# Transposing the doubled attention output once per tile, with the gate weights spread by DMA, in a two-layer Trainium2 block

## The reference

```python
rw = _gating(hidden_states, sim_matrix, gates)        # (b, t, 16)
q = einsum('bte,bted->btd', rw, einsum('btc,ecd->bted', h, q_proj))   # k and v likewise
scores = where(causal, einsum('bqd,bkd->bqk', q, k) * scale, -inf)
attn = einsum('bqk,bkd->bqd', softmax(scores, axis=-1), v)
mixed = attn[:, :, None, :] * rw[..., None]           # (b, t, 16, 64)
return einsum('bted,edc->btc', mixed, o_proj)
```

## Time and profile before

| | |
|---|---|
| median of 3 runs | 1398.0 us (1397.77 to 1398.74) |
| the profiled execution | 1397.29 us, of it 1395.1 us span |
| mean granted clock of PE over the span | 0.972 (1.00 in all of the second layer's tiles past the first) |
| busy over the span | PE 87%, DVE 86%, ACT 79%, POOL 73% |
| first matmul of the tiles | 1093.3 us from the span's start |

### The profile page before, as it was taken

The page is one execution under the profiler, slowest core; times in us unless marked ns, Lnnn a source line. Parts: engine busy times, 40 slices in busy tenths (PEclk is TensorE's granted clock), DMA queues, the critical chain, the costliest instruction groups (busy, mean ns, idle before and its releaser), DMA issues. The chain is left out here.

```text
span 1395.1 us, 24022 instructions
## 1 busy us (share of the span) xinstructions
PE 1208.1 (87%) x8370; PEld 753.3 (54%) x8370; DVE 1196.0 (86%) x1937; ACT 1107.6 (79%) x2031; POOL 1024.6 (73%) x714
## 2 busy tenths in 40 slices
PE   2789999999999999999999999998862599999997
PEld 1344444444454444454444445444431498989897
DVE  5899999999999999999999999999858576767674
ACT  3899999999999999999999999999833455656553
POOL 3689899899989989998998999899942744434320
PEclk9899999999999999999999999999975799999999
DMA  4232111121211112121111212110003876768570
GB/s 112 68 89 66 40 44 52 31 56 44 62 47 39 52 31 57 42 65 51 33 52 31 59 45 61 31 31 1 1 7 55 151 130 120 137 113 146 100 130 10
DMA packets 184598, 86.85 MB, mean 62 GB/s; under 512 B 150176, under 2 KB 166048, under 8 KB 184480
## 3 DMA queue, kind: packets, MB, share of 16 engines
q1 hardware_dynamic: 184480, 85.33, 28.9%
HBM read 7.68 MB, written 2.10 MB: 7 GB/s over the span
## 5 line engine op out<-in xcount | busy, mean ns | idle before, releaser
L490 POOL TENSOR_TENSOR prob<-prob 128x1024 f32<-128x1024 f32 x256 | 604.0, 2359 | 88.4 <-ACT prob L954 72.4
L1245 DVE TENSOR_REDUCE negmax<-score_ps 128x1 f32<-128x1024 f32 x512 | 621.3, 1220 | 35.3 <-PE score_ps L609 26.2
L925 ACT ACTIVATE prob<-score_ps,negmax 128x1024 f32<-128x1024 f32 x512 | 569.8, 1120 | 52.5 <-DVE negmax L1245 47.3
L609 PE MATMUL score_ps<-ka,qa 128*128 128x512 f16 x1024 | 308.3, 383 | 92.6 <-ACT prob L925 81.1
L638 PE MATMUL attn_ps<-probT,v_sb 128*64 128x512 f32 x1024 | 275.9, 618 | 0.8 <-ACT attn_nT L972 0.8
L632 PE MATMUL trans_ps<-ident,prob 128*128 128x128 f32 x2048 | 268.9, 274 | 2.7 <-POOL prob L490 2.7
L632 PEld LDWEIGHTS trans_ps<-ident,prob 128*128 128x128 f32 x2048 | 239.0, 141 | 57.3 <-POOL prob L490 4.0
L557 POOL TENSOR_TENSOR xs<-xnT,rw_all 128x2048 f32<-128x2048 f32 x32 | 117.4, 3671 | 147.3 <-DVE prob L1378 140.5
L488 POOL TENSOR_SCALAR prob<-prob,ccol 128x1024 f32<-128x1024 f32 x192 | 215.0, 1120 | 3.4 <-DVE ccol L1258 3.4
L609 PEld LDWEIGHTS score_ps<-ka,qa 128*128 128x128 f16 x1024 | 88.5, 98 | 211.9 <-ACT prob L925 179.6
L332 DVE COPY probT<-trans_ps 128x512 f32<-128x512 f32 x256 | 174.2, 681 | 3.1 <-PE trans_ps L632 3.1
(11 more groups left out here) (195 smaller groups left out, 1327.9 us busy)
## 6 DMA issues: line engine op xcount, KB each, us to landing
qa<-split SPq DMA_DIRECT2D x256, 64.0 KB, 2.0
ka<-split SPq DMA_DIRECT2D x256, 64.0 KB, 2.0
xg<-xnT SPq DMA_DIRECT2D x16, 512.0 KB, 3.0
resid<-in_L_attn_x SPq DMA_DIRECT2D x4, 512.0 KB, 6.3
wg<-in_L_attn_Wkv SPq DMA_DIRECT2D x32, 64.0 KB, 2.0
out<-prob SPq DMA_DIRECT2D x32, 64.0 KB, 2.5
wg<-in_L_attn_Wq SPq DMA_DIRECT2D x16, 64.0 KB, 1.9
xsT<-prob SPq DMA_TRANSPOSE x64, 4.5
```

The source lines that it names most:

```text
L490: pool.tensor_tensor(prob1[:, n % PROBS, :], prob1[:, n % PROBS, :], prob2[:, n % 4, :], ALU.add).then_inc(mix_ok, 1)
L609: mm = pe.matmul(score_ps[:, sub, kh * HALF:(kh + 1) * HALF], qa[:, par, head * 2 + sub, q0:q0 + P], ka[:, par, head * 2 + sub, kh * HALF: ...
L925: act.activation(prob2[:, n % 4, :] if sub else prob1[:, n % PROBS, :], score_ps[:, sub, :], ACT.Exp, bias=negmax[:, s % 2, sub:sub + 1], ...
L1245: dve.tensor_reduce(negmax[:, s % 2, sub:sub + 1], score_ps[:, sub, :], AX.X, ALU.max, negate=True).then_inc(max_ok, 1)
```

## The change

The mixed rows are formed after the transpose and not before. Once, before the tiles, PE transposes the gate weights of all tokens (four 128x128 transposes), ACT copies them to SBUF (`rwT`), and SP stores them in DRAM (`rw_rows`). For each tile two DMAs load them back so that each of the 128 partitions has the weights of its experts for the tile's 128 tokens (`rw_spread`: 8 groups of two experts; one row is broadcast to 64 partitions). ACT divides the doubled attention output by the sum (`oo`), PE transposes it once, DVE multiplies the transposed output, broadcast to 8 groups, by `rw_spread` (`mT`, 128x1024), and from `mT` ACT takes the high half and DVE the low half in one instruction each.

```diff
+            sp.wait_ge(rwT_ok, 1)
+            sp.dma_start(rw_rows.rearrange("b r q -> r b q"), rwT.rearrange("p (b q) -> p b q", b=B)).then_inc(rwT_out, 16)
+
+            def spread_weights(tile):
+                if tile == 0:
+                    sp.wait_ge(rwT_out, 16)
+                if tile >= 2:
+                    sp.wait_ge(mul_ok, tile - 1)
+                b, t = divmod(tile, NT)
+                rows = rw_rows[b, t * E:(t + 1) * E, :].rearrange("(g two) q -> two g q", two=2)
+                for two in range(2):
+                    sp.dma_start(rw_spread[two * DE:(two + 1) * DE, tile % 2, :, :],
+                                 rows[two:two + 1].to_broadcast([DE, E // 2, P])).then_inc(spread_in[tile % 2], 16)
...
             for tile in range(B * NT + X_AHEAD + PART2_LAG):
                 if tile < B * NT:
                     transpose_x(tile)
+                if 0 <= tile - SPREAD_LAG < B * NT:
+                    spread_weights(tile - SPREAD_LAG)
...
# PE
-                    def m_transposes(bank):
...
-                        for g in range(4):
-                            e = 8 * bank + 2 * g
-                            mm = pe.transpose(t_ps[:, bank, g * P:(g + 1) * P],
-                                              mx[:, v % 2, e:e + 2, :].rearrange("p e d -> p (e d)"), ident[:, :])
-                        mm.then_inc(mT_ps, 1)
...
+                    if live(3):
+                        pe.wait_ge(o_copied, m - 2)
+                        pe.transpose(y_ps[:, P:2 * P], oo[:, (m - 3) % 2, :], ident[:, :]).then_inc(oT_ok, 1)
                     if live(4):
-                        pe.wait_ge(mT_lo, 2 * (m - 3))
...
+                        pe.wait_ge(mT_lo, m - 3)
...
# ACT
             for m in range(X_AHEAD):
                 x_high(m, m % 2)
+            act.wait_ge(rwT_ps, 1)
+            act.activation(rwT, t_ps[:, 0, :], ACT.Copy).then_inc(rwT_ok, 1)
...
+                    if live(3):
+                        act.wait_ge(mul_ok, m - 2)
+                        if m >= 4:
+                            act.wait_ge(y_ok, m - 3)
+                        act.activation(mxT[:, 0, :, :], mT, ACT.Copy).then_inc(mT_hi, 1)
...
+                    if live(2):
+                        act.wait_ge(pv2, m - 1)
+                        act.wait_ge(rec2_ok, m - 1)
...
+                        act.activation(oo[:, m % 2, :].rearrange("p (n d) -> p n d", n=2),
+                                       o2_ps[:, DE:2 * DE].unsqueeze(1).to_broadcast([P, 2, DE]), ACT.Copy,
+                                       scale=rec2[:, m % 2:m % 2 + 1]).then_inc(o_copied, 1)
...
# DVE, between the output and the copy of p2T
+                    if live(3):
+                        dve.wait_ge(oT_ok, m - 2)
+                        dve.wait_ge(spread_in[(m - 3) % 2], 32 * ((m - 3) // 2 + 1))
+                        if m >= 4:
+                            dve.wait_ge(mT_lo, m - 3)
+                        dve.tensor_tensor(mT, y_ps[:, P:2 * P].unsqueeze(1).to_broadcast([P, E // 2, P]),
+                                          rw_spread[:, (m - 3) % 2, :, :], ALU.mult).then_inc(mul_ok, 1)
...
-                        dve.scalar_tensor_tensor(out=mx[:, v % 2, :, :], in0=o2_ps[:, DE:2 * DE].unsqueeze(1).to_broadcast([P, E, DE]),
...
+                        dve.wait_ge(mT_hi, m - 2)
+                        dve.tensor_tensor(mxT[:, 1, :, :], mT, mxT[:, 0, :, :], ALU.subtract).then_inc(mT_lo, 1)
```

More of the change, by code:

```diff
@@ L91 @@
 PART2_LAG = 4
+SPREAD_LAG = 3
 X_AHEAD = 2
@@ L729, in _ @@
             pe.wait_ge(g_V, 2 * B)
+            for b in range(B):
+                mm = pe.transpose(t_ps[:, 0, b * P:(b + 1) * P], rw_all[:, b * NT:(b + 1) * NT, :].rearrange("p t e -> p (t e)"),
+                                  ident[:, :])
+            mm.then_inc(rwT_ps, 1)
             def tiles2(it, first, last):
@@ L737, in live @@
                         return not (first and t < lag) and not (last and t - lag >= NT)
[L739 to L747, removed]
                     def experts(group):
@@ L773, in p_transposes @@
                             return
-                        bank_read(bank, ("y of m - 1",))
+                        if m == 2:
+                            pe.wait_ge(rwT_ok, 1)
+                        else:
+                            pe.wait_ge((pT_A, pT_V)[bank], m - 2)
                         for kb in range(4 * bank, min(v, 4 * bank + 3) + 1):
@@ L1049, in tiles2 @@
                                        accum_out=sum2[:, v % 2:v % 2 + 1]).then_inc(exp2, 1)
[L1050 to L1056, removed]
+                    if live(2):
+                        act.wait_ge(pv2, m - 1)
+                        act.wait_ge(rec2_ok, m - 1)
+                        if m >= 4:
+                            act.wait_ge(oT_ok, m - 3)
+                        act.activation(oo[:, m % 2, :].rearrange("p (n d) -> p n d", n=2),
+                                       o2_ps[:, DE:2 * DE].unsqueeze(1).to_broadcast([P, 2, DE]), ACT.Copy,
+                                       scale=rec2[:, m % 2:m % 2 + 1]).then_inc(o_copied, 1)
                     if live(0):
@@ L1417, in tiles2 @@
                         dve.reciprocal(rec2[:, v % 2:v % 2 + 1], sum2[:, v % 2:v % 2 + 1]).then_inc(rec2_ok, 1)
[L1418 to L1421, removed]
-                        dve.scalar_tensor_tensor(out=mx[:, v % 2, :, :], in0=o2_ps[:, DE:2 * DE].unsqueeze(1).to_broadcast([P, E, DE]),
-                                                 scalar=rec2[:, v % 2:v % 2 + 1],
-                                                 in1=rw_all[:, bass.ds(m - 2, 1), :].rearrange("p a e -> p e a").to_broadcast([P, E, DE]),
-                                                 op0=ALU.mult, op1=ALU.mult).then_inc(mx_ok, 1)
-                    if live(3):
-                        for bank in range(2):
-                            dve.wait_ge(mT_hi, 2 * (m - 3) + bank + 1)
-                            dve.tensor_tensor(mxT[:, 1, 4 * bank:4 * bank + 4, :],
-                                              t_ps[:, bank, :].rearrange("p (g q) -> p g q", g=4),
-                                              mxT[:, 0, 4 * bank:4 * bank + 4, :], ALU.subtract).then_inc(mT_lo, 1)
+                    if live(3):
+                        dve.wait_ge(mT_hi, m - 2)
+                        dve.tensor_tensor(mxT[:, 1, :, :], mT, mxT[:, 0, :, :], ALU.subtract).then_inc(mT_lo, 1)
                     if live(0):
```

28 lines of the change are left out of this document (15 added, 13 removed).

## The result

| | before | after |
|---|---|---|
| median of 5 runs | 1398.0 us (1397.77 to 1398.75) | 1411.3 us (1405.66 to 1413.51) |
| ratio to before, 95% interval | | 1.0085 [1.0064, 1.0105] |
| the profiled execution | 1397.29 us, span 1395.1 | 1413.51 us, span 1411.5 |
| mean granted clock of PE over the span | 0.972 | 0.960 |
| busy over the span | PE 87%, DVE 86%, ACT 79%, POOL 73% | PE 85%, DVE 86%, ACT 79%, POOL 73% |

The kernel became slower, by 13.3 us in the medians: 6.3 us more than the 1405.0 forecast, and within the range of 1397 to 1413, but above the forecast's own range of 1401 to 1409. Its runs also lie 8 us apart, where those of before lie 1 us apart.

What follows compares the result with a forecast made beforehand. Dependency rings between engines, not TensorE's work alone, were taken to bound the kernel. Start 3.3, batch 0 0.5 + 1.08, batches 1 and 2 2 x (1.17 + 1.08), last batch 0.1 - 1.52, tail -1.0: +7.0, 1405.0 us; range 1397 to 1413.

Steps and rivals of the forecast that it cites:

- start: Before the tiles: first DMA transpose 4.1 to 5.3 us late behind the weights copy and store; 3.3 us taken.
- early tiles: Tiles at key blocks v = 0 to 3: y waits for mxT's low half, held by GpSimd; +1.17 us a batch.
- late tiles: Tiles at key blocks v = 4 to 7: 0.87 us of transposes out, 1.14 of product in; net +0.27 us a period.
- last batch: Final batch: early tiles +0.1 us, and TensorE gains 0.76 twice where x_low no longer runs; 0.1 - 1.52.
- tail: After the last experts: the engine chain loses transposes but gains copy waits; -1.0 us (0 to -2).
- o wait: TensorE's wait before the o matmuls at v = 4, 0.37 us before; o was to start 6.4 after experts' end, not 5.2.
- third rival: Tiles at v under 4: if VectorE's signal cannot pass the queued product, o waits; +1.9 us a batch, 1413; chance 0.06.
- the ring: For v of 4 and more: experts' end, x_low, output, copy of p2T, o matmuls; VectorE work before the copy lengthens each period.
- X: The start of x_low, VectorE's low half at L1378; mxT's low half was forecast to end at X + 7.07.
- second rival: Early tiles: GpSimd does not hold mxT's low half, which ends at X + 6.0; 1398.8 us; chance 0.14 for 1396 to 1401.
- TensorE decides: Whole kernel: removing 256 transposes, less 36 new ones, makes it faster, 1377 us; chance 0.12 for 1375 to 1395.
- DMA: Spread-weight loads, 2.5 us a tile, stay hidden; the rival that DMA or SP binds gives 1432 us, chance 0.08.

Runs made afterwards that it cites:

- f2: Changed kernel plus unused filler matmuls on TensorE in the long waits before y at v = 1 and 3 and before o at v = 4 to 7: 1406.74 us.
- the halves alone: Changed kernel with only GpSimd's scaling split into two halves of eight experts, the second after the low half of mxT: 1402.52 us, ratio 1.0041.
- The better version: Changed kernel with product behind the copy of p2T, weights copied before the first high halves, and GpSimd's scaling in two halves: 1386.13 us, ratio 0.9913.
- the two moves: Changed kernel with the product behind the copy of p2T and the copy of transposed weights ahead of the first high halves: 1396.53 us, ratio 0.9988.

## Why the prediction was right, and where its size was off

The working can be set against the profiled execution term by term. Lateness is the start of the last expert matmuls of a period less the same start before; at the end of v = 3 of batch 0 it is 4.40 (1139.77 less 1135.37).

| term | on record | measured | at half clock, on top |
|---|---|---|---|
| start and early tiles of batch 0 | 3.8 | 4.40 | |
| late tiles, batches 0 to 2 | 3.24 | 3.09 | 0.38 |
| early tiles, batches 1 and 2 | 2.34 | 2.34 | 2.81 + 4.49 |
| last batch | -1.42 | -1.07 | |
| tail | -1.0 | -1.2 | 1.22 |
| sum | 7.0 | 7.6 | 8.9 |

7.6 + 8.9 is the 16.4 of the spans to 0.1. The third column is from periods at full clock: 33.41 for the early four (the f2 row) and 40.86 for the late four. The fourth is what the periods of batches 1 (36.22 early) and 2 (37.90) have above that, the 11.13 at v = 7 of batch 0 above 10.75, and the last y:

```profile
1401.02 1.50 PE L813 MATMUL y_ps<-eow_split,mxT 128*128 128x128 f16 x24
1406.47 2.72 PE L813 MATMUL y_ps<-eow_split,mxT 128*128 128x128 f16 x24 [3.95 <-DVE mxT L1447]
```

The stretch at half clock divides into 1.64 us behind the o wait at v = 7 of batch 0 (0.38 there, 1.26 in the period after it, 7.76 instead of 6.50), 1.56 and 2.86 at v = 1 of batches 1 and 2, 1.63 at v = 3 of batch 2 and 1.22 at the last y.

The measured 1411.3 us is outside the forecast's own range of 1401 to 1409. It is inside 1397 to 1413 because that range was stretched to take in the third rival, whose wait did not occur. That the range holds the result is luck; the direction and the two waits are not.

- **Late tiles: right.** Forecast 9.7 at v = 4, measured 9.68, and moving the product out of the ring took the wait away. The product is 1.21 us from start to end, directly ahead of L1433.
- **Early tiles: right.** The low half ends at X + 7.05 at v = 1 (forecast 7.07), and the four periods at full clock give 33.41, the forecast figure to the last digit, which is partly luck: the first is 6.50 and not 6.61, and the new o copy takes 0.35 where the prediction had 0.17. The change does hold the low half, so the second rival falls. Its sum for a low half of 1.2, 31.45, is borne out where GpSimd's work is elsewhere: the four periods of the halves alone give 31.66.
- **Third rival: falls.** DVE's sequencer sent the signal for pT_V (L1436, the first of two in this window) at 1262.9, when x_low (1262.66) had just begun, with the output and the product still ahead of it. So it passes two queued instructions, which agrees with the Trainium skill (Advanced Engine Details and Errata, Engine Queue Depths), and o followed the experts at 1264.34 without a wait.

```profile
L1436 DVEq EVENT_SEMAPHORE  x2: 21/21/21, 1262.9 to 1272.7; - x2
```

- **TensorE decides: falls as a forecast of this kernel.** It is busy 87% of the tiles. The better version shows what part of that rival's gain was real: 11.6 us below the kernel before, once the product, the copy of the weights and GpSimd's work stand elsewhere.
- **DMA: hidden,** as forecast; the loads can go or stay. Without 30 tiles' loads the share is 0.32 less over 271 us, 2.9 us a tile where a share of 1 counts as full. The prediction took 1.25 for the full share, but the rows above read up to 1.35, so its figures in us of full use are rough.
- **Start: 0.6 too small.** The first DMA transpose was issued 5.98 later than before (1090.90 against 1084.92), above the 4.1 to 5.3 of the prediction. The first expert matmul is 5.07 late, of which 4.40 are left at the end of the early tiles.
- **The step that failed** is one of size, in the sum over the early tiles (and, less, over the late tiles and the tail). It priced a longer wait of TensorE at its own length, with the work behind it at the durations of the earlier trace rows, that is at full clock. The runs show TensorE at half clock behind some of these waits. The 1.2 us of the tail, the 7.3 of batches 1 and 2 and the 0.4 of batch 0 were missing, 8.9 in the profiled execution. In the median of five runs it is about 6 us (13.3 less 7.6, an estimate, since only the longest run has a trace), and it varies from run to run, which goes with the spread of 8 us. Filling the waits removed the spread and 4.6 us of the median; 1397.7 + 7.6 + 1.2 + 0.65 = about 1407.1 is what the terms give for that kernel, and 1406.7 was measured.

What stays open is which waits are followed by a fall. With the same wait of 2.75 us at v = 1, some periods have it (after, batches 1 and 2) and one has not (after, batch 3: 9.76); the same holds for the o wait at v = 7 (2.10 us, a fall in batch 0 only) and for the 2.08 us before y at v = 3 (a fall in batch 2, none in batch 1). No run here was made to tell them apart.

## What to carry to other kernels

A wait of the busiest engine costs more than its length when the clock falls behind it: price a lengthened wait once at its length and once with the work after it at the lower clock, and keep both in the range. Before an operand is moved from PSUM to SBUF, look at what GpSimd does at that time; if the instruction then has two SBUF inputs, try the GpSimd work in two parts around it, as here, where that gave 8.8 us alone and 10.4 on top of the two moves. And removing work from an engine that waits gives nothing until the ring of the other engines is shorter: here the same change was 13 us slower or 12 us faster, by where the product, the copy of the weights and GpSimd's scaling stood.

## What the runs showed that I had not expected

- TensorE's granted clock went to 0.50 behind waits of 2.1 to 2.8 us (some of them in two parts with one transpose between) and of 3.95 in the tail, in an otherwise busy stream, but not behind each of them: 24 y matmuls took 2.74 us instead of 1.50, and a period 1.4 to 2.9 us more.
- 36 matmuls of 128x128 without use, 2.34 us of them in a wait of 2.75 us, went with a clock of 1.00 there (y 1.51 us, period 9.76), and fillers in all the waits made the kernel 4.6 us quicker and its runs 0.6 us apart instead of 8.
- A GpSimd scaling in two halves takes 1.90 + 1.90 us instead of 3.61; the 0.2 us more cost nothing, and the kernel before was as fast with it as without.
